# Seven max-pools of two images summed on TensorE, three norms without statistics passes, loads in order of need

## The reference

```python
x = x + block0(_gn(x))  # attention: queries from all pixels, keys and values from a 2x2-strided convolution
x = x + block1(_gn(x))  # four 64-channel chunks: depthwise 3x3 convolution, a linear scan over the pixels, gates, norms
x = x + block2(_gn(x))  # attention among channels: a Gram matrix of the pixels, softmax, projection
x = x + block3(_gn(x))  # adaptive max-pool:
    gap   = mean(x, over pixels)                    # b, c
    score = relu(w2 @ relu(w1 @ gap + b1) + b2)     # b, c
    q_s   = clip(floor(score), 0, 5);  q_b = q_s + 1
    pools = maxpool_same(x, k) for k in (1, 3, 5, 7, 9, 11, 13)
    out   = (score - q_s) * pools[q_b] + (q_b - score) * pools[q_s] + x
```

## Time and profile before

| what | us |
|---|---|
| median of three timed runs | 899.11 |
| lowest, highest | 898.1, 899.64 |
| the profiled execution, its own time | 893.1 |
| its span | 891.3 |
| TensorE (matmul) busy | 668.2 (75%) |
| VectorE busy | 627.6 (70%) |
| ScalarE busy | 389.7 (44%) |
| GpSimd busy | 32.8 (4%) |

### The profile page before, as it was taken

One profiled execution on the slowest core, in us unless ns is written; L12 is line 12 of the kernel. 1 busy time (PEld: TensorE's weight loads), 2 busy tenths in 40 slices (PEclk: granted clock), 3 DMA queues, 4 the chain that ended last, 5 costly groups with the idle time before them and its releaser, 6 DMA issues.

```text
span 891.3 us, 9082 instructions
## 1 busy us (share of the span) xinstructions
PE 668.2 (75%) x3272; PEld 306.1 (34%) x3272; DVE 627.6 (70%) x1117; ACT 389.7 (44%) x623; POOL 32.8 (4%) x26
## 2 busy tenths in 40 slices
PE   2967984997898999999888879886876766387100
PEld 2622532433232354443334442232343222255100
DVE  2555416614958752776788779987889969986897
ACT  0202451558647467556636267715526453101100
POOL 3200000200001000000020000002000000000000
PEclk9965998899998989899989789998895687685655
DMA  8040024000150000004000000020000100001001
GB/s 303 15 122 2 1 68 116 1 1 1 49 135 2 3 0 1 1 1 118 19 1 1 1 1 1 18 78 1 1 1 0 47 1 1 0 0 48 0 0 47
DMA packets 14990, 26.85 MB, mean 30 GB/s; under 512 B 3250, under 2 KB 6994, under 8 KB 14819
## 3 DMA queue, kind: packets, MB, share of 16 engines
q1 hardware_dynamic: 11648, 22.80, 8.6%
q10 hardware_dynamic: 3298, 3.48, 1.3%
HBM read 14.09 MB, written 4.19 MB: 21 GB/s over the span
## 4 chain that ended last, share of the span: by engine, by line
PE 54%; DVE 24%; ACT 13%; issue 4%; SPq 2%; DMA 2%; DVEq 0%; ACTq 0%
PE aD L1517 5%; PE bA L1409 5%; PE aA L1536 4%; DVE NEGMAX L955 4%; PE bA L1550 4%; PE pp L1442 3%; PE aA L1502 3%; PE bA L1638 3%; PE aD L1482 3%; PE aD L1536 3%; ACT PT L503 2%; PE pp L1409 2%; DVE ACC L1280 2%; DVE PA_ L1271 2%; DVE HB L1266 2%
## 5 line engine op out<-in xcount | busy, mean ns | idle before, releaser
L955 DVE TENSOR_REDUCE NEGMAX<-aD 128x2 f32<-128x512 f32 x128 | 82.8, 685 | 34.2 <-PE aD L1482 32.6
L503 ACT ACTIVATE PT<-aA 128x512 f32<-128x512 f32 x128 | 70.2, 594 | 83.4 <-PE aA L1502 82.7
L1482 PE MATMUL aD<-KST,QST 96*128 96x256 f16 x256 | 54.2, 322 | 28.4 <-DVE NEGMAX L955 16.5
L1280 DVE SCALAR_TENSOR_TENSOR ACC<-PA_,COEF,ACC 128x1024 f32<-128x1024 f32 x48 | 61.5, 1282 | 1.2
L1502 PE MATMUL aA<-QST,KST 98*128 98x512 f16 x128 | 47.7, 426 | 13.7 <-ACT PT L503 9.4
L1271 DVE TENSOR_TENSOR PA_<-HB 128x1024 f32<-128x1024 f32 x40 | 49.0, 1225 | 1.0
L1266 DVE TENSOR_TENSOR HB<-PA_ 128x1024 f32<-128x1024 f32 x40 | 48.7, 1217 | 0.1
L1482 PEld LDWEIGHTS aD<-KST,QST 96*128 96x128 f16 x256 | 20.5, 105 | 78.4 <-DVE NEGMAX L955 40.7
L1517 PE MATMUL aD<-PT,VT 128*32 128x512 f32 x256 | 37.8, 665 | 5.0 <-DVE NEGMAX L955 2.0
L790 POOL TENSOR_TENSOR GA<-GA,PT 128x1024 f32<-128x1024 f32 x8 | 19.3, 2428 | 575.0 <-ACT PT L531 575.0
L972 DVE TENSOR_TENSOR GA<-GA,aD 128x512 f32<-128x512 f32 x16 | 10.9, 684 | 41.5 <-ACT GA L516 33.7
(11 more groups left out here) (298 smaller groups left out, 1325.4 us busy)
## 6 DMA issues: line engine op xcount, KB each, us to landing
XF<-in_x SPq DMA_DIRECT2D x4, 1024.0 KB, 5.1
QST<-QH SPq DMA_DIRECT2D x32, 128.0 KB, 2.4
XR<-in_x SPq DMA_DIRECT2D x4, 1024.0 KB, 5.0
out<-ACC SPq DMA_DIRECT2D x4, 1024.0 KB, 4.0
QST<-QL SPq DMA_DIRECT2D x16, 128.0 KB, 2.5
PS<-in_cw ACTq DMA_DIRECT2D x1, 1152.0 KB
WDS<-in_wds SPq DMA_DIRECT2D x1, 1024.0 KB, 8.2
WP<-in_wp SPq DMA_DIRECT2D x2, 256.0 KB, 10.9
```

The source lines that it names most:

```text
L503: e.activation(PROB[:, 4 * kt + j, :], SLOT[f"aA{j % 2}"][:, :], ACT.Exp)\
L955: e.tensor_reduce(NEGMAX[:, h, 2 * j:2 * j + 2], SLOT[f"aD{j % 2}"][:, :].rearrange("p (t k) -> p t k", t=2), AX.X, ALU.max, negate=True). ...
L1280: e.scalar_tensor_tensor(out=acc, in0=interior(PA_, cc), scalar=COEF[:, cc, k:k + 1], in1=acc, op0=ALU.mult, op1=ALU.add).then_inc(*dve_m. ...
L1482: mm = e.matmul(s[:, t * NK:(t + 1) * NK], QST[0:96, h, qt * P:(qt + 1) * P], KST[0:96, h, :], start=True, stop=True)
```

## The change

Three things are changed, and the four orders are new.

1. Images 2 and 3 (`LATE = 2`) get a stream L in place of M. VectorE makes the pools alone, the halves by turns. ScalarE writes 14 diagonal 128 x 128 matrices into a part of `PT` (`DG`), and TensorE sums diagonal times pool in the banks `aA0/1` and `aD0/1`: seven steps for each half, each with two products of 512 columns. ScalarE adds C1 and takes the sums into `ACC`.
2. For norms 1, 2 and 3 `bn_stats` and its small operations go. The residual operations give row sums (`accum_out`), 48 in all, and ScalarE takes the squares with a row sum, 24 operations of 128 x 1024.
3. x comes in two DMAs with a semaphore each; the early weights have four semaphores in the order of their use; ScalarE's 14 DMAs are issued in its set-up, behind the first norm's root. Two of the three folds come ahead of the strided convolution, the rest of the set-up behind the keys. The halves of the queries are computed with the key norm between them, the DMAs to `QST` and `KST` have four semaphores each by the head's place, and scores wait for their own.

```diff
+LATE = 2
+        PART = {s: sb(f"PART_{s}", [P, CC, 2]) for s in "CDM"}
+        DG = PT[:, 0:2, 0:KPOOL * P].rearrange("p c (k n) -> p c k n", n=P)
...
-            sp.dma_start(XF[:, :, :], x_v[:, 0:CC, :]).then_inc(x_loaded, 16)
+            for cc in range(CC):
+                sp.dma_start(XF[:, cc, :], x_v[:, cc, :]).then_inc(x_loaded[cc], 16)
...
+            for loaded, pairs in ((down_loaded, ((COL, cols), (WDS, wds))), (query_loaded, ((WQ, wq),)),
+                                  (kv_loaded, ((WK, wk), (WV, wv))), (mid_loaded, ((WP1, wp1), (WP0, wp0), (XPR, xpr), (DTP, dtp)))):
...
+            def squares(b, l, act, ready, src, junk):
+                MV = GN[GSET[l]][2]
+                for cc in range(CC):
+                    e.wait_ge(*ready[cc])
+                    e.activation(junk(cc), src(cc), ACT.Square, accum_out=MV[:, cc, 1:2]).then_inc(*act.step(f"gn_sq{l}_{cc}"))
+                    yield
...
+            def weights_on_diagonal(b):
+                if b == LATE:
+                    e.wait_ge(*dve_c.at(B - 1, "n1_1"))
...
+                for k in range(KPOOL):
+                    for cc in range(CC):
+                        w = COEF[:, cc, k:k + 1] if k else C0[:, cc:cc + 1]
+                        e.activation(DG[:, cc, k, :], mat("ident"), ACT.Copy, scale=w).then_inc(*act_l.step(f"dg{k}_{cc}"))
+                    yield
+            def pooled_out(b):
+                for cc in range(CC):
+                    e.wait_ge(*pe_l.at(b, f"acc6_{cc}"))
+                    for half in range(2):
+                        e.activation(ACC[:, cc, hs(half)], SLOT[("aA", "aD")[cc] + str(half)][:, :], ACT.Identity, bias=C1[:, cc:cc + 1])\
+                         .then_inc(*act_l.step(f"o{cc}_{half}"))
...
+            def totals(b, l, dve):
+                MV, PART_ = GN[GSET[l]][2], PART[GSET[l]]
+                e.tensor_tensor(MV[:, :, 0], PART_[:, :, 0], PART_[:, :, 1], ALU.add).then_inc(*dve.step(f"gn_m{l}"))
...
-                                           in1=X[:, m, hs(half)], op0=ALU.add, op1=ALU.add).then_inc(*dve_c.step(f"x1_{m}_{half}"))
+                                           in1=X[:, m, hs(half)], op0=ALU.add, op1=ALU.add,
+                                           accum_out=PART["C"][:, m, half:half + 1]).then_inc(*dve_c.step(f"x1_{m}_{half}"))
...
             def widen(b, cc, k):
+                if b >= LATE:
+                    e.wait_ge(*dve.at(b, f"p{k}_0" if cc else f"p{k - 1}_1" if k > 2 else "v1_1"))
...
-                e.wait_ge(*dve_m.at(b, f"acc{k - 1}_{cc}"))
+                e.wait_ge(*(pe_l if b >= LATE else dve_m).at(b, f"acc{k - 1}_{cc}"))
...
+            def stream_l(b):
+                yield from pool_norm(b)
+                yield from pool_score(b)
+                for cc in range(CC):
+                    yield from window3(b, cc)
+                for k in range(2, KPOOL):
+                    for cc in range(CC):
+                        yield from widen(b, cc, k)
```

The last of these is VectorE's; TensorE's is:

```diff
+            def stream_l(b):
+                yield from stream_m(b)
+                for k in range(KPOOL):
+                    for cc in range(CC):
...
+                        e.wait_ge(*act_l.at(b, f"dg{k}_{cc}"))
+                        if k:
+                            e.wait_ge(*dve_l.at(b, f"p{k}_{cc}" if k > 1 else f"v1_{cc}"))
+                        for half in range(2):
+                            mm = e.matmul(SLOT[("aA", "aD")[cc] + str(half)][:, :], DG[:, cc, k, :],
+                                          PA4[:, cc, 1 + 16 * half:17 + 16 * half, 1:1 + W], start=(k == 0), stop=(k == KPOOL - 1))
+                        mm.then_inc(*pe_l.step(f"acc{k}_{cc}"))
```

More of the change, by code:

```diff
@@ L181, in interleave, with images, __init__ @@
         assert next(s, "end") == "end", engine
-def images(stream):
-    for b in range(B):
+def images(stream, first=0, last=B):
+    for b in range(first, last):
         yield from stream(b)
 class Steps:
-    def __init__(self, sem, text, lead=1):
-        self.lead = lead
+    def __init__(self, sem, text, lead=1, first=0):
+        self.lead, self.first = lead, first
         self.sem, self.labels, self.said = sem, text.split(), []
@@ new lines, in stack @@
+                for j in range(4):
+                    for quad in (0, 2):
+                        copy(QST, quad, j, QH)
+                yield
+                sp.wait_ge(*dve_f.at(b, "ql1_0"))
+                for j in range(4):
+                    copy(QST, 1, j, QL)
+                yield
+                sp.wait_ge(*act_f.at(b, "kh1"))
+                copy(KST, 0, 0, KH)
+                copy(KST, 0, 1, KH)
+                sp.wait_ge(*dve_f.at(b, "kl1"))
+                copy(KST, 2, 0, KL)
@@ L393, in max_rows @@
+                copy(KST, 2, 1, KL)
+                for j in (2, 3):
+                    copy(KST, 0, j, KH)
+                    copy(KST, 2, j, KL)
+                yield
             def max_rows(b, g):
@@ L708, in stream_c @@
             def stream_c(b):
+                yield from squares(b, 1, act_c, [dve_c.at(b, f"x1_{cc}_1") for cc in range(CC)],
+                                   lambda cc: XRES[b % 2][:, cc, :], lambda cc: NORM["C"][4][:, cc, :])
                 yield from group_norm(b, 1, act_c, dve_c)
@@ L725, in stream_d @@
             def stream_d(b):
+                yield from squares(b, 2, act_d, [dve_b.at(b, f"x2_{cc}_1") for cc in range(CC)],
+                                   lambda cc: XRES[b % 2][:, cc, :], lambda cc: SQ[:, cc, :])
                 yield from group_norm(b, 2, act_d, dve_d)
@@ L995, in scan_out @@
                     e.scalar_tensor_tensor(out=X[:, m, hs(half)], in0=t, scalar=PB1[:, m:m + 1], in1=X[:, m, hs(half)],
[L996 removed]
+                                           op0=ALU.add, op1=ALU.add,
+                                           accum_out=PART["D"][:, m, half:half + 1]).then_inc(*dve_b.step(f"x2_{m}_{half}"))
                     yield
@@ L1712, in spread_rows, with query @@
                     yield
-            def query(b):
-                for m, half in BLOCKS:
+            def query(b, m):
+                for half in (m, 1 - m):
                     s = take(b, f"pp{1 - half}", dve_f, f"ql{m}_{half}")
```

430 lines of the change are left out of this document (252 added, 178 removed).

## The result

The changed kernel takes 856.44 us (median of 4 executions, 855.57 to 858.21), the kernel before beside it 899.38. The ratio is 0.9523, with a 95% interval of 0.9499 to 0.9548. The forecast was 854.1. That is close, in part by luck: the terms of single stretches missed by up to 9 us, two of them with the wrong sign, and the misses made up for each other in part. In medians the change is 42.9 us, where the sum had 45. The profiled execution took 855.84 us with a span of 853.2, where the sum had 848.1 and 846.3.

A forecast was written before the change was run, and what follows sets the result against it. Neither TensorE nor VectorE bounds the whole: TensorE is 89% busy from 175 to 588 us, VectorE 85% later and alone at the end. Terms sum to -45, so 893.1 becomes 848.1, plus 6.0 gives 854.1 us; range 842 to 866, with rivals 835 to 874.

The forecast's parts named there:

- The start, -9: Up to the first scores: earlier convolution (15.6 to 17.6 us) and fewer DMA issues ahead save 7.6 to 9.6 us, taken as 9.
- Norm 1 of image 0, -5: Norm 1 goes ahead of image 2's statistics: 6.6 us off its path, counted as -5, bounds 0 and -6.6.
- 175 to 588 us, -2: Stretch with TensorE 89% busy: shorter norms against row sums and ScalarE squares, VectorE's relief meeting idle time; -2, bounds -12 and +6.
- 588 us to image 2's residual 3, -4: VectorE loses two norms' statistics, gets 8 row sums and 1.3 us more of image 3's scan; -4, bounds -12 and +2.
- To image 3's residual 2, -11: From image 2's residual 3: image 3's scan is ahead, so its products start 4.2 us behind; -11, bounds -6 and -12.
- To image 3's residual 3, -3: From image 3's residual 2: image 2's sums in TensorE's chain against a higher clock and VectorE's relief; -3, bounds -9 and +5.
- The end, -11: Behind image 3's residual 3: coefficients at 837.8 us, VectorE 33.2 us in place of 46.8, TensorE's sums beside it; -11.
- three signs of being wrong: Last stretch TensorE's at 0.50; image 3's residual 3 over 66 us behind residual 2; a residual operation over 0.3 us longer.
- The row sums, 0.1 us each: Price of row sums in VectorE's 48 residual operations: 0 to 0.19 us each, taken as 0.1.
- R1: Rival: TensorE stays at half clock through the pools, so the end is as late as before; 872 us, chance 0.15.
- R4: Rival: image 2's sums and image 3's channel attention lock TensorE and VectorE at 11 hand-overs; 909 us, chance 0.03.
- The 6.0 us added at the end: Timed median stood 6.0 us above the profiled execution before; the same was added to 848.1, giving 854.1.

The follow-up runs named there:

- the experiment on the loads: Changed kernel with ScalarE's 14 late DMAs issued first and every reader of an early weight waiting for all nine: 859.66 us, ratio 0.9603.
- tail_only: Kernel before with only image 3's pools summed on TensorE by diagonal matrices: 886.54 us, ratio 0.9879.
- old_middle: Changed kernel with each engine's steps from image 2's norm 2 to its residual 3 in the order of before: 871.37 us, ratio 0.9721.
- residual_first: Changed kernel with image 2's last projection and residual 3 ahead of image 3's second centred product, variance and first scaled product: 866.18 us, ratio 0.9675.

## Why the prediction was right, and where it was not

- **The start, -9.** Measured -9.24, but from a convolution at 15.23, earlier than the 15.6 to 17.6 forecast. As a term of the sum it was too large, since the experiment on the loads gives 3.2 us for 6 at the start.
- **Norm 1 of image 0, -5.** The scaling moved by another 9.9 us, outside the bound of -6.6. The trace gives this norm 4.0 us in place of 10.0, near the forecast's path; the other 3.9 us lie ahead of it, and the forecast had no term for them.
- **175 to 588 us, -2.** From norm 1 on it was +4.5, inside the bounds of -12 to +6. VectorE worked 17.1 us less (301.9 before, 284.7 after), TensorE as long as ever (388.8 and 386.3), and so the relief met idle time, as forecast. Yet with the statistics back the kernel was 14.1 us later at 573.9. Both hold: the new order needs the short norms. What gave back 4.5 us wasn't tried.
- **588 us to image 2's residual 3, -4: the step that failed.** Measured +5.4 against the profile of before and +2.0 against `tail_only`'s execution of the same code: outside the bound of +2 or at it, and no shortening in either. The step said "it was busy 115.8 of 133.9 us, so I take -4", and took a busy share for a bound. Its relief came nearly as priced, but by two wrong counts that met: three norms' statistics left VectorE in this stretch, not two, with twelve row sums, not eight, and 3.9 us more of image 3's scan output, not 1.3. VectorE was busy 111.2 us in place of 115.8, and the stretch did not get shorter. In its larger part, the second line of the windows above, VectorE is busy 77.71 of 101.7 us; so there the waits between the engines make the length. No variant of the changed kernel brings it under 135.5 us: 138.8 in the old order, 135.5 with the residual first, 140.1 with the statistics back. What lengthened it stays open. Moving the residual ahead of image 3's products gave 3.8 us, but the whole old order, which has it there too, gave 0.5. The spread rows ran at half clock, 3.64 us in place of 1.95, while the mean clock of the stretch was no lower than before (0.82 and 0.81). The spread rows, first before, then after:

```profile
711.63 1.95 PE L1709 MATMUL pp<-MAT,T 128*32 128x128 f32 x64 [1.12 <-DVE PS L1055]
```

```profile
696.20 3.64 PE L1853 MATMUL pp<-MAT,T 128*32 128x128 f32 x64
```

- **To image 3's residual 2, -11.** Measured -14.1, outside the bound of -12, by the mechanism named: the scan was ahead. `old_middle` and `residual_first` take it away (40.2 and 40.1; 40.4 before). But it belongs with the failed step: together the two were forecast at -15. Against the profile of before they gave -8.7, against `tail_only`'s -15.2. So part of the sum's error in spans is the scatter of before.
- **To image 3's residual 3, -3.** Measured -3.3, and the clock did rise, from 0.69 to 0.95. The term for image 2's sums was too small: without them on TensorE the stretch was 9.2 us longer.
- **The end, -11.** Measured -11.5. The first pool operation starts 8.3 us behind the residual (10.4 before), the sums lie beside the pools, the first one cost VectorE 1.66 us, and no later one cost anything, where the forecast had 1 us for it. None of the prediction's three signs of being wrong came.
- **The row sums, 0.1 us each.** They are instructions of 0.08 us. The rule of the Trainium skill (Vector Engine (DVE) Microarchitecture Reference, section 3.10) agrees with the trace: the read is an instruction of its own.
- **R1.** The Trainium skill (TensorE: Matmul & The Clock Gate, section HAM oscillation — how this bites in real kernels) holds ahead of the first sum (0.50 from 805 to 810 us, TensorE busy 1.22 of 5) and once more within the pools: behind a wait of 2.15 us two sums took 2.92 and 2.66 us, and the clock was 0.66 from 820 to 825. It does not hold for the rest: from 815 to 820 TensorE was busy 3.16 of 5 and kept 1.00, and from 830 us on it had 0.98. So R1's time did not come. R4's lock was not seen: VectorE waited for a sum of image 2 twice, 1.36 and 2.61 us.
- **The 6.0 us added at the end.** As a fixed offset of a profiled execution to the median they were wrong: after, the two differ by 0.6. The profiled 893.1 of before was a draw from the low part of 888.7 to 901.2. But since the sum started from it, adding the 6.0 meant no more than taking the 45 us from the median of before, and there the sum was 2.1 us too large; in spans, against the low draw, it was 6.9.
- **Luck.** In the spans the terms of norm 1 and of image 3's residual 2 were 4.9 and 3.1 us too small, those of 175 to 588 us and of the failed step 6.5 and 9.4 too large. That the total came out close is due to these misses having both signs. The range doesn't follow from the bounds either: added as independent, they give 840 to 869, not 842 to 866.

## What to carry to other kernels

With in-order queues a faster way to compute something is worth what its place in every queue makes of it: the same norms cost 22 us in one order and were worth 23, together with their order, in another. So price an edit together with the order that it comes in, and test it in both. And read a stretch by what is waited for: 85% busy on one engine is no promise that relief of this engine shortens it. Before a miss in one stretch is explained, a second profile of the same code tells how much of it is scatter: here about 3 us in a stretch and up to 8 us at a mark.

## What the hardware showed that was not expected

- Work added to TensorE made its other work faster: with 13 us more of work on it in 62.5 us the granted clock was 0.95 in place of 0.71, and its other products took 9.0 us less.
- Filling TensorE by idle products isn't free. A float32 product of 512 columns takes 0.94 us at full clock (two in the first sum's 1.89), more than its share of gaps of 2 to 4 us, and 8 of them did not hold the clock.
- TensorE can be busy without a rest and still at half clock: from 690 to 700 us in the change it was busy 10.0 of 10 us at 0.50, as the earlier trace rows had shown for 675 to 680.
- The row sum of a VectorE residual operation is read in 0.08 us, that of ScalarE in 0.18 to 0.19.
- The kernel before scatters by 12.5 us over 50 executions (888.7 to 901.2), the changed one by 2.6 over 4. Between two profiles of the same code of before, one mark moved by 8.1 us.
